# One more quad, four plain tiles instead of eight, and a reordered opening in a conditioned residual product

## The reference

```python
def reference(x, cond_1024, L0_cond_weight_matrix, L0_cond_W_proj, L0_cond_b_proj):
    # x: (128, 128, 512), cond: (128, 512), weight_matrix: (1024, 512), W_proj: (512, 512)
    u = gelu(cond @ W_proj + b_proj, approximate=False)
    W_u, W_e = weight_matrix[:512], weight_matrix[512:]
    logits = (u @ W_u)[:, None, :] + einsum('bnd,dc->bnc', x, W_e)
    return x + logits
```

## Time and profile before

| | us |
|---|---|
| median of 3 runs | 347.45 |
| lowest and highest | 347.02, 348.54 |
| the profiled execution | 347.27 |
| its span (first to last instruction) | 345.5 |

### The profile page before, as it was taken

One profiled execution on the slowest core, in us unless ns is written; L12 is line 12 of the kernel. 1 busy time (PEld: TensorE's weight loads), 2 busy tenths in 40 slices (PEclk: granted clock), 3 DMA queues, 4 the chain that ended last, 5 costly groups with the idle time before them and its releaser, 6 DMA issues.

```text
span 345.5 us, 7735 instructions
## 1 busy us (share of the span) xinstructions
PE 340.3 (99%) x2670; PEld 328.6 (95%) x2670; DVE 257.4 (75%) x294; ACT 241.8 (70%) x413; POOL 278.1 (80%) x196
## 2 busy tenths in 40 slices
PE   8999999999999999999999999999999999999996
PEld 4777999999999999999999999999999999999996
DVE  2546997788777778877777887777788777778811
ACT  3361677877777787777778777777877777787751
POOL 0573899888989888898988889898888989888860
DMA  7995679788899778789987888998788899778116
GB/s 268 337 216 140 164 190 255 203 209 198 176 233 229 213 200 208 196 175 235 227 215 200 208 197 174 236 225 217 200 208 197 172 238 227 217 196 211 61 79 228
DMA packets 72264, 70.64 MB, mean 204 GB/s; under 512 B 2880, under 2 KB 67392, under 8 KB 68032
## 3 DMA queue, kind: packets, MB, share of 16 engines
q1 hardware_dynamic: 72256, 70.53, 80.5%
HBM read 36.96 MB, written 33.55 MB: 204 GB/s over the span
## 4 chain that ended last, share of the span: by engine, by line
PE 86%; DVE 1%; issue 0%; ACT 0%
PE banks L731 29%; PE banks L735 28%; PE banks L733 28%; DVE work L511 0%; DVE banks L511 0%; DVE banks L553 0%; ACT snap_rows L465 0%; ACT y L506 0%; DVE y L522 0%; ACT hi L405 0%
## 5 line engine op out<-in xcount | busy, mean ns | idle before, releaser
L731 PE MATMUL banks<-t_hi,hi 128*128 128x256 f32 x480 | 136.0, 283 | 0.2 <-ACT snap_rows L465 0.2
L735 PE MATMUL banks<-t_hi,lo 128*128 128x256 f32 x480 | 135.8, 283 | 0.0
L733 PE MATMUL banks<-t_lo,hi 128*128 128x256 f32 x480 | 135.8, 283 | 0.0
L733 PE MATMUL banks<-w_lo,hi 128*128 128x256 f32 x360 | 101.9, 283 | 0.0
L731 PE MATMUL banks<-w_hi,hi 128*128 128x256 f32 x360 | 101.9, 283 | 0.0
L735 PE MATMUL banks<-w_hi,lo 128*128 128x256 f32 x360 | 101.9, 283 | 0.0
L511 DVE STREAM_TRANSPOSE work<-quad_raw 128x1024 f32<-128x1024 f32 (+1 forms) x60 | 97.3, 1622 | 0.0
L731 PEld LDWEIGHTS banks<-t_hi,hi 128*128 128x128 f32 x480 | 92.1, 192 | 0.6 <-issue 0.6
L733 PEld LDWEIGHTS banks<-t_lo,hi 128*128 128x128 f32 x480 | 92.2, 192 | 0.0
L735 PEld LDWEIGHTS banks<-t_hi,lo 128*128 128x128 f32 x480 | 92.2, 192 | 0.0
L333 POOL TENSOR_TENSOR lo<-work,hi 128x1024 fp32r<-128x1024 f32 x30 | 72.5, 2417 | 23.3 <-ACT hi L397 23.3
(11 more groups left out here) (74 smaller groups left out, 435.8 us busy)
## 6 DMA issues: line engine op xcount, KB each, us to landing
out<-y SPq DMA_DIRECT2D x31, 1024.0 KB, 4.5
quad_raw<-in_x SPq DMA_DIRECT2D x120, 256.0 KB, 5.8
head_raw<-in_x SPq DMA_DIRECT2D x2, 512.0 KB, 5.3
w_e<-in_L_cond_weight_matrix SPq DMA_DIRECT2D x2, 512.0 KB, 5.9
w_proj_sb<-in_L_cond_W_proj SPq DMA_DIRECT2D x1, 1024.0 KB, 9.3
w_u<-in_L_cond_weight_matrix SPq DMA_DIRECT2D x1, 1024.0 KB, 11.1
head_raw<-in_x SPq DMA_DIRECT2D x8, 128.0 KB, 9.4
out<-y SPq DMA_DIRECT2D x3, 256.0 KB, 2.2
```

The lines of the kernel that those rows point to most:

```text
L731: pe.matmul(psum[:, t, :], a_hi[:, 2 * j + t, :], b_hi[:, j, :], start=False, stop=False, skip_group_check=True)
L733: pe.matmul(psum[:, t, :], a_hi[:, 2 * j + t, :], b_lo[:, j, :], start=False, stop=False, skip_group_check=True)
L735: last = pe.matmul(psum[:, t, :], a_lo[:, 2 * j + t, :], b_hi[:, j, :], start=False, stop=(j == T - 1), skip_group_check=True)
```

## The change

- `HEAD_CHUNKS` is 2: four plain tiles, 31 quads. Chunks 2 and 3, their loads, their turns on DVE, their splits and their 48 matmuls of 512 columns are gone; quad 0 starts at tile 4. With an odd number of quads the last one uses buffers number 0.
- SP loads cond and W_proj (now in halves, a semaphore each) first, then x, W_e, x, b_proj, W_u as before, then the first quad in two halves, then the second quad.
- PE: cond is transposed and h computed right after the first idle matmuls; then chunk 0 is transposed, h too, and chunk 0 multiplied. Idle matmuls after the first six: 3 and 2 instead of 8. The bias product stands between the two plain chunks; `DIRECT` is gone.
- The plain chunks' operands lie in `hi` and `lo` number 1, so quad 0 (number 0) has no wait on them. `t_sum` has its own buffer and is computed on DVE (was POOL).
- The PSUM banks of the quads are dealt anew: the seeds of quad 0 that lie in the banks of plain chunk 0 wait for `evacuate(0)` (`seed_c`, `b_seeded`).
- For quad 0, DVE's order is S1, evacuate(0), S2, the rest of S1, S3, evacuate(1); ACT's is up, seed_a, A22, S1, seed_c, S2, S3, S4; POOL splits S2 ahead of forming S4.

```diff
-HEAD_CHUNKS = 4
+HEAD_CHUNKS = 2
-WARM_ON = 8
+WARM_ON = 3
+WARM_LATE = 2
...
+            sp.dma_start(cond_sb[:, :], cond).then_inc(cond_loaded, 16)
+            for n in range(2):
+                sp.dma_start(w_proj_sb[:, 2 * n:2 * n + 2, :],
+                             w_proj_dram[:, 2 * n:2 * n + 2, :]).then_inc(w_proj_loaded[n], 16)
             load_direct(0)
             for n in range(2):
                 load_w_e(n)
             load_direct(1)
-            sp.dma_start(cond_sb[:, :], cond).then_inc(cond_loaded, 16)
-            sp.dma_start(w_proj_sb[:, :, :], w_proj_dram).then_inc(w_proj_loaded, 16)
...
-            load_head(2)
-            load_head(3)
-            load_quad(0, 0)
+            load_first(0)
+            load_first(1)
             load_quad(1, 1)
...
             def period(k, p, first, ahead):
                 act.wait_ge(m1_done, k + 1)
                 if first and p == 0:
-                    act.wait_ge(evacuated, 3)
+                    act.wait_ge(evacuated, 1)
...
+            turn_low(0, 0, True)
+            sum_s1(0, 0, True)
             evacuate(0)
+            sum_s2(0, 0)
+            split_s1(0, 0)
+            sum_s3(0, 0, True)
             evacuate(1)
-            turn_quad(0, 0, True)
-            combine_quad(0, 0, True)
-            evacuate(2)
-            turn_quad(1, 1, True)
-            evacuate(3)
+            turn_up(1, 1, True)
+            turn_low(1, 1, True)
```

More of the change, by code:

```diff
@@ L148, in build_cond_residual @@
         w_u_loaded = sem("w_u_loaded")
-        head_loaded = [sem(f"head_loaded{n}") for n in range(HEAD_CHUNKS)]
+        first_loaded = [sem(f"first_loaded{n}") for n in range(2)]
         quad_loaded = [sem(f"quad_loaded{s}") for s in range(2)]
@@ L354, in _ @@
                     prepare(it * 2 + p, p)
+            prepare(QUADS - 1, 0)
         @block.scalar
@@ L387, in _, with hi_t @@
             last.then_inc(u_ready, 1)
-            head_hi(2)
-            head_hi(3)
+            def hi_t(n):
+                act.wait_ge(t_summed, (1, 3, 2, 4)[n])
+                act.copy(t_hi[:, n, :, :], t_sum[:, n, :, :]).then_inc(t_hi_ready, 1)
+            hi_t(0)
+            for n in range(T, HEAD):
+                direct_hi(n)
+            for n in range(1, 4):
+                hi_t(n)
             def up(k, p, first):
                 act.wait_ge(up_turned, k + 1)
-                if first:
-                    act.wait_ge(multiplied, 2 * p + 1)
-                else:
+                if not first:
                     act.wait_ge(m2_done, k - 1)
+                elif p == 1:
+                    act.wait_ge(multiplied, HEAD_CHUNKS)
                 act.copy(slot(hi[p], UP, 2), a_up[p]).then_inc(up_hi, 1)
@@ L523, in evacuate @@
                                   bias[:, :].unsqueeze(1).to_broadcast([P, T, C]), ALU.add).then_inc(evacuated, 1)
[L525 to L530 removed]
+            by_block = "p (j r) (i m) -> p m j (r i)"
@@ new lines, in raw_tiles, with turn_up @@
+            def raw_tiles(p, n, first):
+                if first and p == 0:
+                    rows = first_half(n)
+                else:
+                    rows = raw_rows(quad_raw[p], QUAD)[:, :, n * T:(n + 1) * T, :]
+                return rows.rearrange("p m n (k j) -> p m j (n k)", k=Q)
+            def turn_up(k, p, first):
+                if first and p == 0:
+                    dve.wait_ge(first_loaded[0], LOADS)
+                else:
+                    dve.wait_ge(quad_loaded[p], (k + p) * (LOADS // 2))
@@ L657, in _ @@
             pe.wait_ge(ident_ready, 1)
+            pe.wait_ge(cond_loaded, 16)
+            flip(flip_psum, by_j(cond_sb[:, :]), cond_flipped)
+            warm(WARM_ON)
+            pe.wait_ge(cond_ready, 1)
+            for j in range(NJ):
+                pe.wait_ge(w_proj_loaded[j // 2], 16)
+                last = pe.matmul(h_psum, cond_t[:, j, :], w_proj_sb[:, j, :], start=(j == 0), stop=(j == NJ - 1))
+            last.then_inc(h_summed, 1)
             for t in range(T):
@@ L716, in _ @@
             last.then_inc(bias_summed, 1)
-            pe.wait_ge(head_lo_ready, 1)
-            *_, last = plain(2)
-            last.then_inc(multiplied, 1)
-            pe.wait_ge(head_lo_ready, 2)
-            pe.wait_ge(bias_ready, 1)
-            *_, last = plain(3)
+            pe.wait_ge(direct_lo_ready, HEAD)
+            for t in range(T):
+                for j in range(NJ):
+                    pe.matmul(banks[1][:, t, :], x_hi[1][:, t, j, :], w_hi[:, j, :], start=(j == 0), stop=False)
+                    pe.matmul(banks[1][:, t, :], x_hi[1][:, t, j, :], w_lo[:, j, :], start=False, stop=False)
+                    last = pe.matmul(banks[1][:, t, :], x_lo[1][:, t, j, :], w_hi[:, j, :], start=False,
+                                     stop=(j == NJ - 1))
             last.then_inc(multiplied, 1)
```

296 lines of the change are left out of this document (134 added, 162 removed).

## The result

The changed kernel takes 349.0 us (median of 14 runs, 347.76 to 350.82) beside 347.26 of the kernel before (14 runs, 347.02 to 348.54): a ratio of 1.0052, 95% interval 1.0040 to 1.0063. It is slower by 1.7 us where 347.1 and no change were forecast. The time is inside the range of 345.0 to 349.5, the sign is not. Two more series of the same file gave 349.44 (ratio 1.0073) and 349.80 (1.0058). Besides the shift there is a spread: the kernel before lies mostly between 347.0 and 347.9, the changed one between 347.7 and 351.5.

The account below looks back on a forecast made before the run. PE's instructions by their pitch, plus opening and stalls, bound the kernel: 347.27 with opening and swap -2.0, new stall +2.05, old stall -0.38, first matmuls +0.07 gives 347.0, against the median 347.1; range 345.0 to 349.5 us.

Parts of the forecast that it names:

- part 2: Opening up to chunk 0, with cond and W_proj loaded first: chunk 0 moves by 3.3 us, opening gains 1.2 us.
- it lands at 9.9: Opening: W_e's first half, now fifth transfer, lands at 9.9 us, as cond with the same bytes did before.
- W_proj's split into two transfers: Opening loads, a bound on what the trace doesn't show: the split costs 0 to 0.4 us, one DMA's issue.
- bound for a longer lag: Opening, W_e's landing: were its lag half as long again as cond's, +0.45 us.
- The stall at M6(0): Quad 0: PE waits 2.05 us for ACT's seed of b_bank before M6, where before there was no stall.
- `snap2`'s wait: M7 of quad 0: the old 0.38 us stall goes, since ACT has snap2 at 36.0 and M7 needs it at 36.6.
- two chains end together: M1 of quad 1: POOL's upper blocks allow 38.0, PE arrives at 38.01 after its stall; within 0.1 us.
- clock falls in the new stall: Rival, slower: PE's clock drops in quad 0's new wait for ACT's seed; chance 0.07.
- further stalls: Rival, more small stalls: chains 2% longer at quad 1's two tight waits add 0.3 to 1.0 us; chance 0.17.
- the one at M6(0) was there: Answers the faster rival that quad 0's seed stall is absent: 345.0, or 346.0 with half the gain; chance 0.18.
- the first clock rival: Rival, clock (slower), its details cut from the text given; chance 0.14.
- h from 6.0 to 9.4: Opening, PE: h's eight records by 0.43 us, 3.43 us, run until 9.4, ahead of chunk 0.

Follow-up runs that it names:

- half of W_proj: Changed kernel without the load of W_proj's second half, h using the first half twice: median 348.81 us, 9 of 11 runs at a clock of 0.995.
- the first quad turned round: Changed kernel with ACT's seed and snapshots earlier, PE's M7 before M3 and POOL's splits reordered in quad 0: 346.73 us, ratio 0.9983; repeats 346.97 and 346.85.

## Why the forecast was wrong, and where it was right

- **The step that failed** is the landing of W_e's first half in part 2, "it lands at 9.9", and with it the bound given for "W_proj's split into two transfers: from 0 to 0.4 us, the issue of one DMA". I read bytes and lag from a queue in which W_proj was one transfer, and priced the split by SP's time to issue it. With it undone W_e is used at 9.56 to 9.85 in three traces; with it, at 10.50 to 13.05 in eight, as bytes flow slower (225 to 252 GB/s up to 8.72 us, for 267 to 270) and W_e lands later behind them. The term is mis-sized by 0.6 to 3.2 us. The forecast's own bound for a longer lag, +0.45, had no room for it.
- **The stall at M6(0)**: 2.05 forecast, 1.97 measured; `snap2`'s wait is gone; M1(1) came 10.83 after M1(0), forecast 10.7. That two chains end together was shown by removing one (+0.0) and both (-1.45).
- **A rival that holds in part**: "clock falls in the new stall", given 0.07. It is no either-or. It happened in 32 of the 62 runs of all versions that have this stall, and in none of the 94 of those that don't and in whose traces PE stands nowhere for 2 us; it costs 1.5 us. My 2.4 us for it (349.5) was an estimate: that PE goes at half its pace for 4.9 us, as long as it does at the start of the kernel before, from 1.2 to 6.1. There six idle matmuls of 512 columns start 0.43 us apart, and those from 6.16 on 0.215 apart. The low stretch was 3.4 us, at a granted clock of 0.50.
- **The other rivals**: no further stalls came, and the one at M6(0) was there. The slow pitch of the start, on which the first clock rival (0.14) was built, was no cause in the profiled run: h took 3.77 us from 5.87 on, its first matmuls 0.43 apart. But its end differs from run to run: in five other traces h took 4.07 to 4.25 us, with its first two matmuls 0.85 to 0.98 apart, for 3.67 where they were 0.43 apart. Behind a late W_e that is hidden; with half of W_proj, where h binds, M1(0) moved from 27.25 to 27.99, 0.5 of it by this. The granted clock stands as 1.00 even there, so a mean of 0.995 doesn't come from the start.
- **h from 6.0 to 9.4** is a term of the opening sum. No run shows the clock of PE that its start at 6.0 takes for granted: the granted clock reads 1.00 over the opening of all twenty traces. What they show is pitches. In the first trace of the changed kernel six idle matmuls start at 1.20, four transposes at 3.73, three idle ones at 4.59, 0.43 apart, and h at 5.87. The transposes are 0.21 to 0.22 apart between 4.7 and 5.7 us and 0.11 apart at 11.8 (before), as the 0.11 in chunk 0 has it.
- **The sum**: the changed kernel's 31 runs have a median of 349.32. With W_proj in one transfer and full clock it is 347.5 (four runs), against 347.1 forecast; the 0.4 fits h waiting for W_proj's landing (0.62 in the one trace, of a run at 0.995), but no trace of these four shows it. The forecast's own last step is 0.1 short: 347.01 and 0.18 are 347.2. The runs with two transfers and full clock have a median of 348.62 (19 runs), so 1.1 us is the split's. 12 of the 31 runs lose 1.5 us by the clock, 0.6 on the mean. 347.5 + 1.1 + 0.6 is 349.2.
- **Open**: why the split makes the flow slower. Each half gives a partition 4 KB in one piece, the whole gives it 8 KB; whether the length of the pieces or the number of transfers does it wasn't tried. Open too is why the clock falls in some runs with the stall and not in others.

## What to carry to other kernels

A transfer that is split so that its consumer can start early can also change how all that is queued behind it lands, and by more than the issue of one DMA: here splitting 1 MB in two cost what comes next 1.1 us in the median, and undoing it, with the first quad turned round as well, brought runs within 0.9 us of one another. Where a profiled run is good and the median isn't, look at the granted clock of every run before looking for another wait: a stall can be priced right and still bring a second cost in half of the runs. And where two chains end together, cut both or neither.

## What was not expected of the hardware

- TensorE's clock fell behind an idle stretch of 2.0 us, in 32 of 62 runs. In the three traces that show it the engine began at a granted clock of 1.00 and slowed 0.7 to 1.5 us later, to 0.50 for 3.4 us, and rose to 1.00 again with PE at work. In the stretch of 4.25 us it fell while the engine still stood (5 of 5 runs, one traced). Versions whose longest stretches are 2.2 and 2.3 us had 1 of 5 and 2 of 5 runs at 0.995; no trace shows where it fell in those. Eight matmuls of zeros in the gap of 2.0 us kept the clock up in 12 of 12 runs, and in 12 of 12 with half of W_proj, where 9 of 11 had fallen without them.
- DVE's fourth sum of `t_sum` took 1.67 us in place of 0.69, and POOL's split beside it 1.62 in place of 1.28, in this trace and in all sixteen others where POOL's first split of `t_sum` starts beside the sums:

```profile
18.86 1.62 POOL L311 TENSOR_TENSOR t_lo<-t_sum,t_hi 128x512 fp32r<-128x512 f32 x1 [17.38 <-ACT t_hi L380]
```

```profile
18.63 0.69 DVE L626 TENSOR_TENSOR t_sum<-w_e,t_sum 128x512 f32<-128x512 f32 x1
19.36 1.67 DVE L628 TENSOR_TENSOR t_sum<-w_e,t_sum 128x512 f32<-128x512 f32 x1
```

  It reads as if each had waited for the other: POOL for the end of the sum before, DVE then for POOL's end at 20.48. These two sums are the only DVE instructions with two operands in SBUF beside POOL's work; the splits and sums of the quads read one operand from a bank, and keep their 0.68. In the two versions where POOL's splits start only after the four sums (x and half of W_e first; b_proj late), the fourth takes 0.69 as well. It was hidden here under the bias product.
